# Rotary pairs swapped by a VectorE shuffle instead of by a second projection, with the sine product and the sum on GpSimd

## The reference, cut to what matters

```python
def _rope(x, sin, cos):
    s = sin[None, None]; c = cos[None, None]
    xe = x[..., ::2]; xo = x[..., 1::2]
    re = xe * c - xo * s
    ro = xe * s + xo * c
    return jnp.stack((re, ro), axis=-1).reshape(x.shape)

def _attn(xq, ctx, wq, wkv, wo, bo):
    q = _heads(xq @ wq)
    k, v = jnp.split(ctx @ wkv, 2, axis=-1)
    ...
    q = _rope(q, sq, cq); k = _rope(k, sk, ck)
    sim = jnp.einsum('bhnd,bhmd->bhnm', q, k) * DH ** (-0.5)
    a = jax.nn.softmax(sim, axis=-1)
    o = jnp.einsum('bhnm,bhmd->bhnd', a, v)
```

## Time and profile before

| | |
|---|---|
| median of 3 runs | 5964.02 us (5939.23 to 5966.58) |
| the profiled execution, its own time | 5934.54 us |
| its span, first to last instruction | 5932.8 us |
| mean granted TensorE clock, as a share of full speed | 0.955 |
| busy: TensorE (PE) matmuls, VectorE (DVE), ScalarE (ACT), GpSimd (POOL) | 91%, 74%, 57%, 43% |

### The profile page before, as it was taken

How to read it: one execution, slowest core, us unless ns; L and a number is a source line. 1 busy time by engine, 2 the same in 40 slices (tenths; PEclk the granted TensorE clock), 3 DMA queues, 4 the chain that set the end, 5 groups by cost and what they waited for, 6 DMA issues and landing times. The chain is left out here.

```text
span 5932.8 us, 167110 instructions
## 1 busy us (share of the span) xinstructions
PE 5411.6 (91%) x66584; PEld 3112.1 (52%) x66584; DVE 4361.4 (74%) x6682; ACT 3379.4 (57%) x7674; POOL 2532.9 (43%) x2193
## 2 busy tenths in 40 slices
PE   5899999999998999999899899999989999999967
PEld 4554555545455455555545456455554545555442
DVE  6888776667888867576887886667788787767633
ACT  3455566565565566656455565665546556665634
POOL 2643544444343444544444344445434445444420
PEclk9999999999999999999999999999989999999975
DMA  4010010101001000010101101010100100101000
GB/s 105 12 40 16 15 29 14 32 12 40 18 17 43 14 26 19 22 24 17 43 13 32 25 14 33 11 34 14 36 21 14 38 17 19 25 14 31 10 17 6
DMA packets 282358, 145.85 MB, mean 25 GB/s; under 512 B 151517, under 2 KB 266813, under 8 KB 281470
## 3 DMA queue, kind: packets, MB, share of 16 engines
q1 hardware_dynamic: 281598, 135.17, 9.5%
HBM read 112.39 MB, written 3.01 MB: 19 GB/s over the span
## 5 line engine op out<-in xcount | busy, mean ns | idle before, releaser
L2032 ACT ACTIVATE probs<-ring 128x512 f32<-128x512 f32 (+1 forms) x4096 | 2084.0, 571 | 1245.9 <-PE ring L1535 1234.8
L2394 DVE TENSOR_REDUCE max_part<-ring 128x2 f32<-128x800 f32 (+2 forms) x2304 | 2257.5, 1009 | 687.2 <-PE ring L1535 678.1
L1511 POOL TENSOR_TENSOR weight_sum<-weight_sum,probs 128x512 f32<-128x512 f32 (+1 forms) x1408 | 1812.7, 1287 | 208.6 <-ACT probs L2032 68.4
L1511 POOL TENSOR_TENSOR weight_sum<-probs 128x512 f32<-128x512 f32 x256 | 331.6, 1295 | 2169.5 <-ACT probs L2032 1639.7
L1535 PE MATMUL o_acc<-probs,region 128*64 128x256 f32 (+1 forms) x6656 | 894.8, 389 | 3.4 <-issue 2.2
L1535 PE MATMUL ring<-qop,region 64*128 64x256 f16 x9984 | 790.4, 274 | 23.5 <-ACT probs L2032 6.9
L1535 PEld LDWEIGHTS ring<-qop,region 64*128 64x128 f16 x9984 | 454.3, 96 | 247.1 <-issue 114.4
L1535 PEld LDWEIGHTS o_acc<-probs,region 128*64 128x64 f32 (+1 forms) x6656 | 415.2, 136 | 280.7 <-issue 120.7
L1535 PE MATMUL ring<-shift_q,shift_k 64*128 64x256 f16 (+1 forms) x3840 | 535.1, 273 | 0.0
L2418 DVE RECIPROCAL o_inv<-ring 128x256 f32<-128x256 f32 x256 | 447.7, 1749 | 116.1 <-PE ring L1535 115.9
L1535 PE MATMUL o_acc<-probs,x_nv 128*32 128x256 f32 x6656 | 483.4, 407 | 27.6 <-ACT probs L2032 26.7
(11 more groups left out here) (191 smaller groups left out, 6935.7 us busy)
## 6 DMA issues: line engine op xcount, KB each, us to landing
stage<-in_wide SPq DMA_DIRECT2D x448, 64.0 KB, 2.0
nk<-x_nk SPq DMA_DIRECT2D x768, 25.0 KB
wo_stage<-in_wide SPq DMA_DIRECT2D x32, 512.0 KB, 4.0
ff_w<-in_ff_w SPq DMA_DIRECT2D x48, 256.0 KB, 3.0
stage<-in_wide SPq DMA_DIRECT2D x64, 128.0 KB, 2.6
v_stage<-in_wide SPq DMA_DIRECT2D x128, 64.0 KB, 1.9
ff_w<-in_ff_w SPq DMA_DIRECT2D x16, 512.0 KB, 3.6
v_stage<-kv_split SPq DMA_DIRECT2D x128, 48.0 KB, 1.7
```

The costliest lines, as they stand in the source:

```text
L1511: pool.tensor_tensor(total, before, probs[0:rows_, (un.chunk + k) % PROBS, :], ALU.add)\
L2032: act.activation(to, src, ACT.Exp, scale=t.scale).then_inc(exp_done.sem, 1)
L2394: dve.tensor_reduce(dst, src, AX.X, ALU.max).then_inc(*release(one))
```

## The change

There is one "op" job and one product per rotary operand. VectorE copies it out of the bank with the partitions exchanged in pairs (`stream_shuffle` with the mask `PARTNER`) into `swapped`, and multiplies the bank with the cosines into `raw`. GpSimd multiplies `swapped` with the sines, in place, and adds it to `raw`; then ScalarE and VectorE make the high and the low part as before. `raw` and `swapped` have two slots each. The second sets of weights are no longer loaded, nor split and stored at the start. The plan has the new steps and new costs for them, and the orders of all engines come out anew.

```diff
     def wide_jobs(self):
         def op(o):
-            return [("op", o, r) for r in range(2 if self.rope else 1)]
+            return [("op", o, 0)]
...
             if t.rope:
-                if k == 0:
-                    at = ROPE_OPS.index((n, i))
-                    before = ROPE_OPS[at - 2] if at >= 2 else None
-                    deps = [("DVE", ("job", before[0], low_job(UNITS[before[0]].t, before[1])))] if before else []
-                    self.part("DVE", "rope", due, one, 0.03 + w * 0.00142, [pe, *deps])
-                    return
-                self.part("DVE", "rope", (due[0], due[1] - 0.5), ("sin", n, j), 0.03 + w * 0.00142, [pe])
-                self.part("DVE", "rope", due, one, 0.05 + w * 0.00142, [("DVE", ("sin", n, j)), ("DVE", ("job", n, j - 1))])
...
+                first = due[0], due[1] - 0.5
+                self.part("DVE", "rope", first, ("swap", n, j), 0.13 + w * 0.00142, [pe, *swapped])
+                self.part("DVE", "rope", due, ("cos", n, j), 0.03 + w * 0.00142, [pe, *free])
+                self.part("POOL", "rope", first, ("sin", n, j), 0.08 + w * 0.0025, [("DVE", ("swap", n, j))])
+                self.part("POOL", "rope", due, one, 0.08 + w * 0.0025, [("POOL", ("sin", n, j)), ("DVE", ("cos", n, j))])
+            self.part("ACT", "op", due, one, 0.17 + w * 0.00083, [("POOL", one) if t.rope else pe])
...
         elif kind == "low":
-            self.part("DVE", "low", due, one, 0.16 + w * 0.00105, [("ACT", ("job", n, op_job(t, i)))])
+            dur = 0.52 + w * 0.0008 if t.rope else 0.16 + w * 0.00105
+            self.part("DVE", "low", due, one, dur, [("ACT", ("job", n, op_job(t, i)))])
...
+PARTNER = [p ^ 1 for p in range(32)]
...
+                    if one[0] == "sin":
+                        a0 = 0 if i == 0 else un.t.kc[i - 1][0]
+                        pool.wait_ge(pair_swapped.sem, pair_swapped.at(un.n, un.t.rank(i) + 1))
+                        pool.tensor_tensor(swapped[:, z, 0:w], swapped[:, z, 0:w], rope_sin[:, a0:a0 + w], ALU.mult)\
+                            .then_inc(sin_ready.sem, 1)
+                        return
+                    pool.wait_ge(*taken(one))
+                    pool.wait_ge(sin_ready.sem, sin_ready.at(un.n, un.t.rank(i) + 1))
+                    pool.tensor_tensor(raw[:, z, 0:w], raw[:, z, 0:w], swapped[:, z, 0:w], ALU.add)\
+                        .then_inc(rope_step.sem, 1)
...
                         if old:

                             dve.wait_ge(rope_step.sem, rope_step.at(old[0].n, old[0].t.rank(old[1]) + 1))
-                        dve.tensor_tensor(raw_sin[:, 0:w], v, rope_sin[:, a0:a0 + w], ALU.mult)\
-                            .then_inc(*release(made))
+                        dve.stream_shuffle(swapped[:, z, 0:w], v, PARTNER).then_inc(pair_swapped.sem, 1)
                         return
...
-                    dve.tensor_tensor(turned, turned, raw_sin[:, 0:w], ALU.add).then_inc(rope_step.sem, 1)
+                    if old:
+
+                        dve.wait_ge(rope_low.sem, rope_low.at(old[0].n, old[0].t.rank(old[1]) + 1))
+                    dve.tensor_tensor(raw[:, z, 0:w], v, rope_cos[:, a0:a0 + w], ALU.mult).then_inc(*release(made))
```

More of the change, by code:

```diff
@@ L455, in holds @@
     if kind == "op" and t.rope:
-        return "DVE", one if k == 0 else ("sin", one[1], j)
+        return "DVE", ("cos", one[1], j)
     if kind == "op":
@@ L1008, in build @@
         n_t = sb("n_t", [D, 2, N])
[L1010 removed]
+        stage = sb("stage", [P, 2, W_COLS])
         v_stage = sb("v_stage", [P, 2, P])
@@ L1019, in build @@
         weight_sum = sb("weight_sum", [P, 2, N])
-        raw = sb("raw", [P, 2, ROPE_COLS])
-        raw_sin = sb("raw_sin", [P, ROPE_COLS])
+        raw = sb("raw", [P, ROPE_SLOTS, ROPE_COLS])
+        swapped = sb("swapped", [P, ROPE_SLOTS, ROPE_COLS])
         max_part = sb("max_part", [P, 4, 8, 4])
@@ L1101, in build @@
         o_copied = per_unit("o_copied", lambda un: 1)
-        stage_in = [per_unit(f"stage_in{z}", lambda un, z=z: (48 if un.t.rope else 32) * (un.t.wide and un.wide_at % 2 == z))
+        stage_in = [per_unit(f"stage_in{z}", lambda un, z=z: 32 * (un.t.wide and un.wide_at % 2 == z))
                     for z in range(2)]
@@ L1520, in divide, with turn @@
                         .then_inc(wide_out.sem, 1)
+                def turn(one):
+                    un, i = UNITS[one[1]], UNITS[one[1]].t.jobs[one[2]][1]
+                    z, w = raw_slot(un, i), N if i == 0 else un.t.kc[i - 1][1]
+                    if one[0] == "sin":
[8 more added lines that the diff above has]
+                        .then_inc(rope_step.sem, 1)
                 for one in ORDER_OF["POOL"]:
@@ L1524, in program @@
                         pre(one)
+                    elif one[0] in ("sin", "job"):
+                        turn(one)
                     elif one[0] == "scale":
@@ L1733, in wide_job @@
                     elif kind == "op" and i == 0:
-                        last = mm_64(out[:, 0:N], stage[:, w_at, k, W_Q:W_Q + P], h_t[:, u % 2, :], True, True)
+                        last = mm_64(out[:, 0:N], stage[:, w_at, W_Q:W_Q + P], h_t[:, u % 2, :], True, True)
                     elif kind == "op":
@@ L1738, in wide_job @@
                             halves = k_split_of(un)
-                            last = in_halves(out[:, 0:w], [halves[:, k, l, :] for l in range(2)],
+                            last = in_halves(out[:, 0:w], [halves[:, l, :] for l in range(2)],
                                              [src[:, l, a0:a0 + w] for l in range(2)], mm_64)
                         else:
-                            last = mm_64(out[:, 0:w], stage[:, w_at, k, W_K:W_K + P], src[:, a0:a0 + w], True, True)
+                            last = mm_64(out[:, 0:w], stage[:, w_at, W_K:W_K + P], src[:, a0:a0 + w], True, True)
                     elif kind == "val":
```

76 lines of the change are left out of this document (32 added, 44 removed).

## The result

The changed kernel takes 6081.65 us (median of 4 runs, 6073.43 to 6092.49) against 5954.52 for the kernel before (4 runs): a ratio of 1.022, 95% interval 1.020 to 1.024. It is **slower** by 127 us where 5770 was forecast. Its profiled span is 6080.6 us, 147.8 longer than before's.

The account below looks back on a forecast made before the run. VectorE and TensorE were taken to bound rotary phases: 7.4 us (self) plus 15.6 (cross, less 8 GpSimd overhang) gives 23 per phase, 184 in eight, plus 1 at the start; 5750 profiled, 5770 predicted, range 5630 to 5915.

Parts of the forecast that it names:

- forecast of -207: VectorE, rotary phases: the sum's 300.8 us go, low parts cost 94 more; net 207 us less, 26 per phase.
- The shuffle, taken at 499 ns: VectorE, rotary operands: the shuffle replacing the sine product costs the same 499 ns, since it computes nothing.
- The low parts were to grow by 94 us: VectorE, rotary operands: the low parts' extra time grows with GpSimd's share, from 42% to 74%; 448 x 0.21 = 94 us.
- overhang at units 3 and 4: Cross part, successive wide units: GpSimd's new passes exceed its holes by 5 us, at two or three places; 8 us per phase.
- five at TensorE's, 5 x 3.34 = 16.7: Cross part of each rotary phase: five of eight units run at TensorE's pace and gain 3.34 us each, 16.7 us.
- the comparison with plain phases: Rotary phases take 49 and 51 us more than plain ones; TensorE's busy time makes 38.4 and 36.7 of that.
- The regimes of the earlier trace: Rotary phase: self part with both engines near their limit, early cross part at VectorE's pace, later both at their limit.
- Plain phases stay at 321 and 343: Phases with the plain wide layer: their times stay at 321 and 343 us after the change.
- GpSimd's turn in the chain makes it slower: Rival, rotary operand chain: waits for GpSimd's sum expose 6 us per cross unit, 1.5 per self unit; +195, 6150 us; chance 12%.
- three signs that were to show me wrong: TensorE's waits for maxima grow, VectorE waits over some 100 us for GpSimd, or the rotary phases' clock falls below 0.95.

Follow-up runs that it names:

- thin_gpsimd: Changed kernel with GpSimd's sine product and sum cut to 16 columns each, orders and all other work kept; 5957.14 us, 0.998 to 1.002 of the kernel before.
- vector_turns: Changed kernel with the sine product and the sum moved from GpSimd to VectorE, orders planned anew; 6289.59 us, 1.053 to 1.059 of the kernel before.
- lighter_both: Kernel before, orders untouched, both projections of the rotary layer's context operands made of one f16 product instead of three; 5963.28 us, ratio 0.999 to 1.003.
- turns_first_30_thin: turns_first_30 with GpSimd's rotary passes cut to 16 columns; 5913.91 us, 0.991 to 0.995 of the kernel before.
- turns_first_30: Changed kernel with GpSimd's rotary passes due 15 us earlier and the wide rotary cross unit's due time 30 instead of 28; 5995.69 us, ratio 1.004 to 1.010.
- lighter_second: Kernel before, orders untouched, only the second projection of the context operands cut to one of three f16 products; 6005.62 us, ratio 1.005 to 1.011.
- run 63: A count, not a label: the kernel before, unchanged, was executed 63 times beside the experiments; 5934 to 5983 us.

## Why the prediction was wrong, step by step

- **VectorE**: net -239 us of busy time against a forecast of -207. Two terms erred in opposite ways, and a third was missing. The shuffle, taken at 499 ns, has a mean of 0.54 us (0.445 for 256 columns, 0.609 for 400), +18 us. The low parts were to grow by 94 us with GpSimd's share; they fell from 335 to 326 us. Scaling with GpSimd's share was wrong. A low part waits if a GpSimd pass is under way when it starts: before, 78 of the 192 of 400 columns did, and took 1.23 us on average, the other 114 took 0.57. In the changed kernel more do, 112, but they wait less, 0.97 us against 0.57, since most of the passes that they meet are the new ones, shorter than an addition. These two terms would make -292; the other 53 us had no term, among them 18 of the normalisation pass `xn`, 10 of the maxima and 6 of the mask loads. By the Trainium skill (VectorE: DVE Perf Modes, the perf-mode tier table) the shuffle was an estimated 0.47 us for 400 columns; the trace has 0.61, and decides.
- **GpSimd**: 831 us in 896 passes against 835. By the Trainium skill (GPSIMD Engine Reference, Elementwise — side-by-side cycle accounting) it was an estimate of 666; the rows decide. What its time cost was priced at 8 us a phase, 64 in all, as an overhang at units 3 and 4; measured 125 on the given orders, 82 on better ones, and not at that place, where the values ran faster than before. Which wait it is that carries GpSimd's time to the end stays open.
- **The step that failed** is the sum: "five at TensorE's, 5 x 3.34 = 16.7" us in the cross part of each phase, 134 in all, TensorE's saved busy time taken as time, with no term for the idle time and the lower clock that come with it. In the eight rotary phases these took back 107 and 115 of the 285 us without GpSimd's time (thin_gpsimd), 162 and 200 with it. On two orders the whole saving was worth 51 and 75 us, and on the orders of before 237 us less gave nothing and 119 less a loss of 49. The ground for it, the comparison with plain phases, was no comparison of one variable: a plain phase also has less VectorE work (68% busy against 83%), and vector_turns and the moved sum point to this as worth time, with new orders in both. The regimes of the earlier trace rows were read as fixed; but the 0.83 and 0.89 in them were a warning: in the kernel before, too, TensorE had lost clock where VectorE set the pace.
- **"Plain phases stay at 321 and 343"** failed too: 331 and 353. No term stood for the new plan. Due times alone gave 86 us back, 53 of them in the plain phases, and the control shows 75 us from one planned cost. But plain phases also lengthen without a new plan, by 25 us in lighter_both and 36 in heavier_second, and why is open.
- **The rival that won**, "GpSimd's turn in the chain makes it slower", had the right sign and 12%, but nothing shows that its path is what cost. The wait that it named (the third shuffle for GpSimd's sum) was found, 110 us in all; with it gone, by a third slot and a new plan, nothing was gained, and the waits for maxima at its end are as long without GpSimd's time (156 us against 161). Its size, 195, was too large, and without GpSimd's time there is still no gain on these orders. That the sign came right is luck in part. Of the three signs that were to show me wrong, all came: waits for maxima grew, VectorE's waits for GpSimd are over 100 us, and the clock of rotary phases is below 0.95.

The account, by the ratios and a time of before of 5955 us: forecast -184. With better orders and without GpSimd's time the change brought -44 (turns_first_30_thin, 0.9926); GpSimd's time makes it +43 (turns_first_30, 1.0073); the orders that the plan gave make it +133 (1.0223; +127 by the medians). So 140 us of the forecast gain were never in TensorE's and VectorE's saved time, 87 are GpSimd's and 90 the orders'. The last two depend on which is taken first: by thin_gpsimd GpSimd's time is 125 and the orders 43.

**Open.** Why the granted clock falls in one rhythm and not in another was not settled: lighter_second (119 us less, slower) and lighter_both (237 us less, same) can't be ordered by the amount of work. Nor is it known why plain phases grow in kernels whose plain work and orders are those of before, nor by which wait GpSimd's time counts. What the 10.2 us wait at the start of a rotary phase costs was not tried by itself; the run with a third slot, which has no such waits, gained nothing.

## What to carry to other kernels

Busy time taken from the busiest engine is not time: put it back (do the work twice) or take it out alone on unchanged orders before believing in it; here 285 us were worth 51 to 75. Where a planner lays out the order anew, run a control that changes only a planned cost, since its spread (here 1.3%) can be larger than the change. Compare a mean clock over several executions, since one execution of the same kernel can stand at its edge. A wait that a list names is not yet a cost: here 86 us of such waits went and the time stayed. And of a change with several parts try each alone: with the sum moved alone the kernel was 0.3 to 0.9% faster, and the rest of the change lost more than that.

## What the runs showed of the hardware

- With every order kept, 119 us less work on TensorE lowered its granted clock from 0.950 to 0.935 (means of all executions on one chip; 0.955 to 0.934 in the profiled ones), and the kernel got 49 us slower. The Trainium skill (TensorE: Matmul & The Clock Gate, Terms) prices time at the low level at the share of the pulses left out, half. The trace agrees roughly: 129 us more of clock cost less 119 of work would make 10, and the busy time rose by 30.
- The same program, run 63 times, stood at clocks of 0.944 to 0.957 and took 5934 to 5983 us; for each 10 us of clock cost the time was 7 us longer.
- A VectorE pass with two SBUF inputs waits for a GpSimd pass that is under way. Of the 78 low parts of 400 columns that met one in the kernel before, each took what was left of the pass and 0.44 us more (the others 0.57 in all); the cosine product out of PSUM took 0.56 us either way.
- A shuffle of pairs of partitions out of PSUM costs 8 to 9% more than a plain pass (609 against 558 ns for the cosine product of 400 columns, 445 against 412 for 256); the load of its mask shows as 0.01 us.
- A GpSimd pass with two SBUF inputs of 16 columns took 0.24 and 0.29 us on average (thin, better orders), so about three quarters of the 1.0 us of 400 columns are by the column.
